# Two transposing DMAs a slot and an output product in fp16 halves, in layer 0 of a two-layer transformer kernel

## The reference, cut to what matters

```
N_HEADS = 32; N_KV_HEADS = 8; HEAD_DIM = 64; SLIDING_WINDOW = 64
qkv = einsum('bsd,od->bso', x, w_qkv)                 # 256 -> 2048 + 512 + 512
q, k, v = split(qkv, ...)                             # 32 query heads, 8 key/value heads
q = _rms_norm(q, q_norm_w); k = _rms_norm(k, k_norm_w)
q, k = _rope(q, k)
scores = einsum('bhqd,bhkd->bhqk', q, k_rep) * HEAD_DIM ** -0.5
scores = scores + _sliding_mask(s, s, 0)              # keys q-63 .. q
probs = softmax(scores)
attn = einsum('bhqk,bhkd->bhqd', probs, v_rep)        # each key head serves 4 query heads
return einsum('bso,do->bsd', attn, w_out)             # 2048 -> 256
```

## Time and profile before

| | us |
|---|---|
| three runs | 1151.46, 1159.83, 1161.42 (median 1159.83) |
| the profiled execution, time | 1153.36 |
| its span, first to last instruction | 1151.4 |
| PE busy | 1083.7 (94%) |
| DVE, ACT, POOL busy | 720.0, 669.9, 709.8 |
| mean granted clock of TensorE, share of full speed | 0.963 |

### The profile page before, as it was taken

How to read it: one execution, slowest core, us unless ns; L and a number is a source line. 1 busy time by engine, 2 the same in 40 slices (tenths; PEclk the granted TensorE clock), 3 DMA queues, 4 the chain that set the end, 5 groups by cost and what they waited for, 6 DMA issues and landing times. The chain is left out here.

```text
span 1151.4 us, 25288 instructions
## 1 busy us (share of the span) xinstructions
PE 1083.7 (94%) x8217; PEld 626.9 (54%) x8217; DVE 720.0 (63%) x1496; ACT 669.9 (58%) x1639; POOL 709.8 (62%) x1003
## 2 busy tenths in 40 slices
PE   4999999999999999999999999388999999999989
PEld 2577767767767766767776776153222222333224
DVE  5765555555655655655546544446999999888911
ACT  2544545455455555545544544005999999888970
POOL 4887787877877777777777775421565664332230
PEclk9999999999999999999999999767999999999995
DMA  6432212212212212212212111341111211112001
GB/s 214 112 78 50 55 34 46 51 35 49 50 36 50 46 39 50 47 39 49 47 39 46 38 39 35 111 117 18 21 33 26 30 30 30 39 34 29 7 2 36
DMA packets 149220, 55.74 MB, mean 48 GB/s; under 512 B 131108, under 2 KB 147428, under 8 KB 148580
## 3 DMA queue, kind: packets, MB, share of 16 engines
q1 hardware_dynamic: 146596, 49.68, 19.5%
q10 hardware_dynamic: 2496, 4.46, 1.1%
HBM read 18.49 MB, written 4.19 MB: 20 GB/s over the span
## 5 line engine op out<-in xcount | busy, mean ns | idle before, releaser
L1233 DVE TENSOR_REDUCE l_mxv<-l_mx 128x1 f32<-128x1024 f32 x256 | 295.0, 1218 | 33.8 <-PE l_mx L1419 33.7
L1144 ACT ACTIVATE l_prob<-l_sc 128x512 f32<-128x512 f32 x512 | 272.8, 606 | 21.6 <-PE l_sc L1427 20.4
L541 DVE TENSOR_TENSOR t<-qk,tcw 128x320 f32<-128x320 f32 x128 | 62.9, 491 | 263.7 <-ACT v L369 263.0
L458 ACT ACTIVATE probs<-sc,neg_bound 128x512 f32<-128x512 f32 x128 | 87.9, 687 | 229.0 <-PE sc L858 229.0
L659 POOL TENSOR_TENSOR t<-t 128x320 f32<-128x320 f32 x128 | 110.7, 865 | 149.3 <-DVE t L542 148.7
L1419 PE MATMUL l_mx<-l_kt,l_qt 48*128 48x512 f16 x512 | 156.5, 388 | 14.8 <-DVE l_mxv L1233 13.5
L1427 PE MATMUL l_sc<-l_qt,l_kt 50*128 50x512 f16 x512 | 156.5, 383 | 0.8 <-ACT l_prob L1144 0.8
L1398 PE MATMUL l_acc<-l_prob,qkv_all 128*17 128x256 f32 x2048 | 155.0, 387 | 0.0
L650 POOL TENSOR_TENSOR rm<-ss,half_neg 128x5 f32<-128x5 f32 x128 | 152.0, 1188 | 0.0
L816 PE MATMUL pv<-v,probs 128*128 128x65 f32 x1024 | 141.9, 282 | 0.0
L844 PE MATMUL ob<-wo,ats 128*128 128x256 f32 x512 | 131.9, 380 | 0.5 <-ACT ats L369 0.5
(11 more groups left out here) (173 smaller groups left out, 2112.0 us busy)
## 6 DMA issues: line engine op xcount, KB each, us to landing
v<-v SPq DMA_DIRECT2D x240, 16.2 KB, 1.8
qkv_all<-w_qkv SPq DMA_DIRECT2D x3, 768.0 KB, 8.6
xn_all<-xs SPq DMA_DIRECT2D x16, 128.5 KB, 2.1
xa<-x SPq DMA_DIRECT2D x16, 128.0 KB, 2.3
wo<-w_o SPq DMA_DIRECT2D x2, 1024.0 KB, 8.7
qt<-nat SPq DMA_TRANSPOSE x128, 2.4
xc<-x SPq DMA_DIRECT2D x16, 128.0 KB, 2.3
out<-xc SPq DMA_DIRECT2D x16, 128.0 KB, 2.0
```

The source lines that it names most:

```text
L1144: act.activation(prob[:, (y * NI + u) % NPR, h * 512:(h + 1) * 512], sc[:, k % NSC, :], ACT.Exp, scale=D1 ** -0.5).then_inc(s_["act_sc"], 1)
L1233: dve.tensor_reduce(mxv[:, x % 2, u:u + 1], mx[:, MX[k] % 2, :], AX.X, ALU.max).then_inc(s_["dve_mx"], 1)
```

## The change

Both transposes of PE go. The key head joins the four query heads in one transposing DMA of six 128-column blocks: block 0 holds the key's hi part twice, block 1 its lo part and zeros, blocks 2 to 5 the queries. It lands in `tk`, three buffers, behind 64 columns that ACT copies in from `kcs`, where it keeps the last 64 key columns of each head; both copies of ACT stand at lag 6. The attention output is split into fp16 hi and lo (`an16`: hi by ACT, lo by DVE) and turned by a second transposing DMA of four blocks, at lag 9. The output product moves to lag 10 and uses fp16 parts: for each of two column halves hi x hi, hi x lo and lo x hi, each as two matmuls of 64 output rows. The output weights are scaled by 64 and the values by 8, and the residual sum divides by it. The weights are loaded in fp32 into space that the first weights have left, and split into `wo_hi` (ACT) and `wo_lo` (DVE) in slots 9 to 16.

`qk` has two buffers, and PE waits for the group before the last. The values move in groups of two and four instead of one, so that SP starts fewer of these DMAs. POOL subtracts for the four query heads only, and does so ahead of its addition; DVE does it for the key head. ACT's blocks of lag 9 and lag 5 stand ahead of those of lag 4. The steps after each tile move by one slot.

```diff
-LAG_W = 9
-WD_K = 2
+LAG_W = 10
+WD_K = 1
...
 
-    return (n + 2) * G + 7 if n >= NT - 2 else (n + 3) * G + 4
+    return (n + 3) * G if n >= NT - 2 else (n + 3) * G + 4
...
-        wo = sb("wo", [P, G, 2, D])
+        wo_hi = sb("wo_hi", [P, G, 2, D], F16)
+        wo_lo = sb("wo_lo", [P, G, 2, D], F16)
...
+        nat = sb("nat", [P, 2, NB, P], F16)
+        tk = sb("tk", [P, NQ, NB, WIN + P], F16)
+        kcs = sb("kcs", [P, B, G, 2, WIN], F16)
...
+        an16 = sb("an16", [P, 2, 2, 4, HD], F16)
+        ats = sb("ats", [P, NA, 2, 2, P], F16)
...
-        qk = ps("qk", [P, 512])
+        qk = ps("qk", [P, 2, 512])
...
-                if s in (LAG_A + 1, LAG_A + 3):
-                    j = (s - LAG_A) // 2
-                    sp.dma_start(wo[:, j * 4:j * 4 + 4, :, :], w_o[:, j * 4:j * 4 + 4, :, :]).then_inc(wo_ld[j], 16)
+                if s in (LAG_A + 2, LAG_A + 6):
+                    j = (s - LAG_A) // 4
+                    sp.wait_ge(s_["dve_wq"], j * 4 + 4)
+                    for k in range(j * 4, j * 4 + 4):
+                        sp.dma_start(wq_f[:, :, k, 0:D], w_o[:, k, :, :]).then_inc(wo_ld[j], 16)
...
                 n, k, ok = at(s, LAG_A + 1)
-                if ok:
+                if ok and k % 2 == 1:
 
                     sp.wait_ge(s_["act_A"], n * G + k + 1)
                     wait(sp, s_["pe_V"], (n - B) * G + k + 1)
-                    sp.dma_start(v0[WIN:P, n % B, k, :], v1[0:WIN, n % B, k, :]).then_inc(vnw[k], 16)
+                    sp.dma_start(v0[WIN:P, n % B, k - 1:k + 1, :], v1[0:WIN, n % B, k - 1:k + 1, :]).then_inc(vnw[k // 2], 16)
+                n, k, ok = at(s, LAG_O)
+                if ok:
+
+                    m = n * G + k
+                    sp.wait_ge(s_["dve_al"], m + 1)
+                    wait(sp, s_["pe_W"], m - NA + 1)
+                    sp.dma_start_transpose(ats[:, m % NA, :, :, :].rearrange("p l a t -> p (l a) t"),
+                                           an16[:, m % 2, :, :, :].rearrange("p l i d -> p (l i d)")).then_inc(at_ld[m % NA], 16)
                 n, k, ok = at(s, LAG_N)
                 if ok:
 
                     m = n * G + k
+                    sp.wait_ge(s_["dve_kl"], m + 1)
                     sp.wait_ge(s_["pool_lo"], m + 1)
                     wait(sp, s_["pe_S"], m - NQ + 1)
-                    sp.dma_start_transpose(qt[:, m % NQ, :, :], nat[:, k % 2, 0:REP, :].rearrange("p r d -> p (r d)")
+                    wait(sp, s_["act_kt"], m - NQ + 1)
+                    sp.dma_start_transpose(tk[:, m % NQ, :, WIN:WIN + P], nat[:, k % 2, :, :].rearrange("p j d -> p (j d)")
                                            ).then_inc(turned[m % NQ], 16)
...
+                n, k, ok = at(s, LAG_O)
+                if ok:
+
+                    m = n * G + k
+                    act.wait_ge(s_["dve_an"], m + 1)
+                    if m >= 2:
+                        act.wait_ge(at_ld[m % NA], 16 * (m // NA))
+                    ev(an16[:, m % 2, 0, :, :], an[:, m % 2, :, :]).then_inc(s_["act_an"], 1)
+                n, k, ok = at(s, LAG_N)
+                b = k % 2
+                if ok:
+                    act.wait_ge(s_["pool_v"], n * G + k + 1)
+                    landed(act, n * G + k - 2)
+                    ev(nat[:, b, 0, :].rearrange("p (j d) -> p j d", j=2), t1[:, b, 0:1, :].broadcast_to([P, 2, HD])
+                       ).then_inc(s_["act_kh"], 1)
+                    ev(nat[:, b, 2:NB, 0:HD], t1[:, b, 1:NH, :]).then_inc(s_["act_hi"], 1)
                 k = s - LAG_A + 2
                 if 0 <= k < G:
                     act.wait_ge(wq_ld[part_of(WQ_PARTS, k)], 16)
                     ev(wq_hi[:, :, k, :], wq_f[:, :, k, :], WS).then_inc(s_["act_wq"], 1)
...
+                if 0 <= k < G:
+                    act.wait_ge(wo_ld[k // 4], 16 * 4)
+                    ev(wo_hi[:, k, :, :], wq_f[:, :, k, 0:D], WS).then_inc(s_["act_wo"], 1)
...
                 n, k, ok = at(s, LAG_A)
...
-                    ev(v1[:, n % B, k, 0:HD], qk[:, NH * HD:CW], 1.0 / WS).then_inc(s_["act_A"], 1)
-                n, k, ok = at(s, LAG_O)
-                b = k % 2
-                if ok:
-                    act.wait_ge(s_["pe_O"], n * G + k + 1)
-                    wait(act, s_["pe_W"], n * G + k - 1)
-                    ev(ats[:, b, :, :, :].rearrange("p a h q -> p h a q"), atv).then_inc(s_["act_at"], 1)
-                n, k, ok = at(s, LAG_N)
-                b = k % 2
-                if ok:
-                    act.wait_ge(s_["pool_v"], n * G + k + 1)
-                    wait(act, s_["pe_T"], n * G + k - 1)
-                    landed(act, n * G + k - 2)
-                    ev(nat[:, b, :, 0:HD], t1[:, b, :, :]).then_inc(s_["act_hi"], 1)
+                    ev(v1[:, n % B, k, 0:HD], qk[:, k % 2, NH * HD:CW], VS / WS).then_inc(s_["act_A"], 1)
                 n, k, ok = at(s, LAG_T)
-                if ok and n >= B:
-
-                    act.wait_ge(s_["pe_S"], (n - B) * G + k + 1)
-                    ev(kts[:, n % B, :, k, 0:WIN], kts[:, n % B, :, k, P:P + WIN]).then_inc(s_["act_kc"], 1)
+                if ok:
+
+                    m = n * G + k
+                    wait(act, s_["pe_S"], m - NQ + 1)
+                    if m == 0:
+                        act.wait_ge(s_["set_k"], 1)
+                    ev(tk[:, m % NQ, 0:2, 0:WIN], kcs[:, n % B, k, :, :]).then_inc(s_["act_kc"], 1)
+                    landed(act, m)
+                    act.wait_ge(s_["act_kc"], m + 1)
+                    ev(kcs[:, n % B, k, :, :], tk[:, m % NQ, 0:2, P:P + WIN]).then_inc(s_["act_kt"], 1)
                 c = (s - LAG_F0) % 16 // 2
                 i = (s - LAG_F0) // 16
                 if s >= LAG_F0 and s % 2 == LAG_F0 % 2 and c < NF and i < NI:
...
-                    dve.tensor_tensor(xc[:, par, :], ob[:, 0:D], xc[:, par, :], ALU.add).then_inc(s_["dve_x1"], 1)
+                    dve.scalar_tensor_tensor(xc[:, par, :], ob[:, 0:D], OS, xc[:, par, :], ALU.mult, ALU.add
+                                             ).then_inc(s_["dve_x1"], 1)
+                n, k, ok = at(s, LAG_O)
+                if ok:
+
+                    m = n * G + k
+                    dve.wait_ge(s_["act_an"], m + 1)
+                    dve.tensor_tensor(an16[:, m % 2, 1, :, :], an[:, m % 2, :, :], an16[:, m % 2, 0, :, :], ALU.subtract
+                                      ).then_inc(s_["dve_al"], 1)
+                n, k, ok = at(s, LAG_N)
+                b = k % 2
+                if ok:
+
+                    dve.wait_ge(s_["act_kh"], n * G + k + 1)
+                    dve.tensor_tensor(nat[:, b, 1, 0:HD], t1[:, b, 0, :], nat[:, b, 0, 0:HD], ALU.subtract
+                                      ).then_inc(s_["dve_kl"], 1)
...
-                n, k, ok = at(s, LAG_A)
-                b = k % 2
-                if ok:
-
-                    pool.wait_ge(s_["dve_A"], n * G + k + 1)
-                    pool.tensor_tensor(t1[:, b, :, :], t1[:, b, :, :], t2[:, :, :], ALU.add).then_inc(s_["pool_u"], 1)
                 n, k, ok = at(s, LAG_N)
                 b = k % 2
                 if ok:
 
                     pool.wait_ge(s_["act_hi"], n * G + k + 1)
-                    wait(pool, s_["pe_T"], n * G + k - 1)
                     landed(pool, n * G + k - 2)
-                    pool.tensor_tensor(nat[:, b, :, HD:P], t1[:, b, :, :], nat[:, b, :, 0:HD], ALU.subtract
+                    pool.tensor_tensor(nat[:, b, 2:NB, HD:P], t1[:, b, 1:NH, :], nat[:, b, 2:NB, 0:HD], ALU.subtract
                                        ).then_inc(s_["pool_lo"], 1)
                 n, k, ok = at(s, LAG_A)
                 b = k % 2
                 if ok:
 
...
-                    wait(pe, s_["act_A"], n * G + k)
-                    wait(pe, s_["dve_A"], n * G + k)
...
-                n, k, ok = at(s, LAG_O)
-                b = k % 2
-                if ok:
-                    pe.wait_ge(s_["dve_an"], n * G + k + 1)
-                    t, j, ahead = at(s, LAG_S + 1)
-                    if ahead:
-                        pe.wait_ge(s_["act_exp"], t * G + j + 1)
-                    wait(pe, s_["act_at"], n * G + k)
-                    for h in range(2):
-                        ins = pe.transpose(atv[:, h, :, :], an[:, b, h, :, :], idf[:, :])
-                    ins.then_inc(s_["pe_O"], 1)
                 f = (s - LAG_F0) % 16 // 2
...
-                n, k, ok = at(s, LAG_T)
-                b = k % 2
-                if ok:
-                    if n == 0 and k == 0:
-                        pe.wait_ge(s_["set_dve"], 1)
-                    pe.wait_ge(s_["pool_lo"], n * G + k + 1)
-                    wait(pe, s_["act_kt"], n * G + k)
-                    for j in range(2):
-                        for a in range(2):
-                            ins = pe.transpose(tr[a * HD:(a + 1) * HD, j, :], nat[:, b, REP, j * HD:(j + 1) * HD],
-                                               idh[:, :])
-                    ins.then_inc(s_["pe_T"], 1)
...
```

(19 more changed lines are left out.)

131 lines of the change are left out of this document (66 added, 65 removed).

## The result

The changed kernel takes 1166.4 us (median of four runs, 1161.6 to 1168.9) against 1155.6 for the kernel before (four runs, 1142.4 to 1161.4). The ratio is 1.0144, 95% interval 1.0081 to 1.0207: slower, since the whole interval lies above 1, though its lower end is under the 1% that the prediction took as what a measurement can tell. 1146 us was forecast. The profiled execution took 1168.9 us (span 1167.0), 15.6 us more in span than the one of before.

A forecast was written before the change was run, and what follows sets the result against it. PE bound the old kernel; after the change a ring through ACT, DVE and POOL would, at about 5.3 us a slot. Start +9, the laps after it -14, end -2 gave -7: 1153.4 to 1146 us, range 1126 to 1178.

The forecast's parts named there:

- PE as the bound, and what comes off it: PE sets layer 0 at 5.45 us a slot; without transposes and with a 0.84 us output product its period becomes 77.6.
- serial products: Rival: the output product's 64-row matmuls run one after another, 5.49 us a slot on PE, 1172 us in all; chance 0.13.
- a late landing: Rival: the transposing DMAs queue up and land over 5.0 us after issue, so ACT waits; about 1180 us; chance 0.12.
- a ring that doesn't bind: Rival: PE stays the bound at 4.85 us a slot, about 1097 us in all; chance 0.08.
- The ring: Once-a-slot loop of ACT's copies, DVE's products, POOL's addition, power and multiplication: a lap cannot be under 5.0 us (sum 5.04).
- What was added to 16 bare laps: Per 16 slots, 2.1 us for ACT's layer 1 evacuations, 1.4 for POOL's rotation, 1.3 chosen for unpriced steps: 84.8 us.
- Idle of PE within a slot is some 1 us at most, so I expect none: PE's waits in layer 0 stay short, so no granted clock below 1.00 between 100 and 700 us.
- The start: First to 14th square: laps that also hold ACT's weight casts take 72.7 us against 63.5, +9.2 us.
- The end: Last group's road to its output product: longer by the DMA, shorter by two transposes and a copy; -4 to +3, taken as -2.
- Sum: Whole kernel: 9 - 14 - 2 = -7 us, from 1153.4 us in the profiled execution to 1146.
- The forecast's own range: Whole kernel if the forecast case holds, with a slot of about 5.3 us: 1130 to 1160 us; chance 0.62.
- 0.06 for "slower" within this case: Of the forecast case's 0.62: 0.24 faster by over 1%, 0.32 within 1%, 0.06 slower.

The follow-up runs named there:

- The extra copy on and off it: The changed kernel with one more unread ACT copy a slot: ahead of the square (on the ring) 1187.0 us, behind the value copy (off it) 1164.2 us.
- The filled kernel: The changed kernel with 12 more unused PE matmuls in the one slot of eight where PE waits for DVE's division: 1158.4 us, ratio 1.0078.
- without the casts: The changed kernel with ACT's casts of the weights moved from ahead of the square to behind the value copy: 1163.4 us, ratio 1.0172.
- the kernel before with its ring closed and POOL's remainder first: The kernel before with only ACT's nat copy moved ahead of its square and POOL's remainder ahead of its addition: 1177.4 us, ratio 1.0248.
- the opened kernel with the rotation dealt out: The changed kernel with ACT's nat copies behind its value copy, POOL's addition ahead of its remainder, layer 1's rotation over three slots: 1119.6 us, 0.9759.

## Why the prediction was wrong, point by point

- **PE as the bound, and what comes off it.** Right. PE's period without waits is 77.3 us (said 77.6), the output product 0.78 (said 0.84). The rivals of serial products, of a late landing and of a ring that doesn't bind are out.
- **The ring.** Right in place and size: 4.98 us a lap (said 5.04), 85.4 us for a period (said 84.8). The extra copy on and off it shows that it is a cause and not a coincidence. What was added to 16 bare laps came out right by luck. Read from the laps of the last period, the two with the rotation have 2.6 us more than the shortest (said 1.4), the six with ACT's evacuations 2.9 (said 2.1), and the rest 0.3 (1.3 was chosen).
- **"Idle of PE within a slot is some 1 us at most, so I expect none" of a lower clock.** This step failed, and with it a term that was put at nothing. It took PE's idle time as the mean of a slot, 5.3 - 4.85. The rotation comes all at once in one slot of eight: the laps with it are 6.6 or 6.0 us in place of 5.0, PE waits 2.0 to 2.7 us in one piece, and in seven of twelve cases the clock falls. The filled kernel puts this at 5 to 9 us, 8 against the changed kernel's own profile. Of the 11 us by which the middle missed, about 3 are left, which the period's 0.6 us over 6.4 periods covers.
- **The start.** The lap and its casts are where the prediction had them, but +14.3 was measured against +9.2. The term that was too small is POOL's part of the lap. The prediction took the power at its steady 1.18 us and the multiplication at 0.72. In the first 13 laps the powers take 18.6 us together instead of 15.3 and the multiplications 11.1 instead of 9.4, which is the missing 5.0. In the kernel before, the same steps took 0.4 and 1.1 us more than that, but on no ring. The long ones stand beside DVE's split of the weights, one in the second lap:

```profile
26.94 1.44 DVE L518 SCALAR_TENSOR_TENSOR wq_lo<-qkv_all,wq_hi 128x768 f16<-128x768 f32 x1
...
27.52 1.90 POOL L694 TENSOR_TENSOR rm<-ss,half_neg 128x5 f32<-128x5 f32 x1
```

  That DVE's work is the reason was not shown by a run. Nor is the sum of the lap the only bound there: without the casts, which the sum gives 7.7 us (5 x 0.73 + 8 x 0.5), the laps are 2.3 us shorter. What stands close behind them wasn't tried.
- **The end.** The output product's road gained 0.1 us and not 2. Layer 1 took 4.4 us more with the same code. In the 17 profiles of kernels that differ only in layer 0 it took 408.0 to 421.3 us, at granted clocks of 0.92 down to 0.89, and the kernel before with its ring closed and POOL's remainder first has the longest. I can't tie this to the change; that a change in layer 0 moves it was not shown.
- **Sum.** -7 became +15.6: 5 us at the start, 8 by the clock, 3 to 4 by the period and the rotation, 2 at the end, 4 in layer 1.
- **The chances.** 1166 us lies inside the stated range of 1126 to 1178, but only in the part kept for serial products and late landings, and neither took place. The forecast's own range, 1130 to 1160, was missed. With a ring only 0.5 us a slot under the old bound, and a start that gives most of it back, the forecast was a small difference of large terms. The terms that were missing or short all had the same sign, and 0.06 for "slower" within this case was too little.

Where did PE's 0.6 us a slot go? In the closed ring nearly all of it into waits for the ring, and what was left into the clock and the start. In the opened kernel with the rotation dealt out, about two thirds arrive: 87.2 to 80.7 us a period, of 77.3 possible.

## What to carry to other kernels

When work is taken off the bounding engine, look in the new order of the other engines for a loop from one slot to the next: an instruction that waits for another engine's end, with an input of that engine's next turn behind it. Then add up bounds by slots, not by means: a burst of 2 us once in eight slots that a slack bound swallows becomes a wait in one piece under a tight one. A ring is a floor under every slot, so it takes away the short slots in which a busier engine catches up. The repair is in the order, not in less work: two copies behind two others (with the small moves on DVE and POOL that go with them) and one rotation in three slots turned +1.4% into -2.4%.

## What the runs showed of the hardware that was not expected

- The granted clock fell to its lower level, 1.2 GHz, after a PE wait of 2.7 us (0.50 over the next 4.8 us, rows above), but neither every time nor for the same time. After 2.66 us that ended at 187.84 it stayed at 1.00 (rows above), and after 2.67 us that ended at 362.77 the window of the next 5.2 us is at 0.67:

```profile
362.80:368.00 5.20, 5.20 (x32) 3.03 (x33) 3.52 (x14) 2.35 (x8) 3.61 (x5) 0.67 0.41 69
```

- Useless PE work of 29 us made layer 0 5 to 9 us faster, while the granted clock from 200 to 650 us went from 0.96 to 1.00.
- Fp16 matmuls with 64 stationary columns each, in pairs that write the lower and the upper 64 rows of one PSUM tile, accumulate at one pair per 0.11 to 0.13 us, about the pace of one matmul of 128 stationary columns (0.12 us, 516.71 to 516.83 in the earlier trace rows).
- POOL's power of 128x5 elements took 1.18 us in the steady state and 1.67 to 1.95 us in five of the first 13 laps of the changed kernel.
